# Routed experts of a preLN block: token rows kept as fp16 halves, results scattered by choice, down products in fp16

## What is computed

```python
x = x + attention(layernorm(x))
flat = layernorm(x)                                    # 2048 x 512
_, topk_idx = top_k(flat @ router_w + router_bias, 4)
comb = the 4 softmax scores of a token, divided by their sum
g = silu(einsum('nd,edf->nef', flat, wg))              # f = 128
u = einsum('nd,edf->nef', flat, wu)
routed = einsum('ne,nef,efd->nd', comb, g * u, wd)
x = x + routed + shared                                # shared: 2 dense experts of width 512
```

## Time and profile before

| | us |
|---|---|
| median of 3 runs (lowest, highest) | 1158.7 (1157.71, 1162.43) |
| the profiled execution | 1163.25 |
| its span, first to last instruction | 1161.4 |
| PE busy | 1090.9 (94%) |
| DVE busy | 818.3 (70%) |
| ACT busy | 571.3 (49%) |
| POOL busy | 458.5 (39%) |

### The profile page before, as it was taken

The page is one execution under the profiler, slowest core; times in us unless marked ns, Lnnn a source line. Parts: engine busy times, 40 slices in busy tenths (PEclk is TensorE's granted clock), DMA queues, the critical chain, the costliest instruction groups (busy, mean ns, idle before and its releaser), DMA issues.

```text
span 1161.4 us, 29336 instructions
## 1 busy us (share of the span) xinstructions
PE 1090.9 (94%) x9641; PEld 493.2 (42%) x9641; DVE 818.3 (70%) x1324; ACT 571.3 (49%) x1123; POOL 458.5 (39%) x591
## 2 busy tenths in 40 slices
PE   5995899999999998899999999999999999998998
PEld 3533233333333332455444544544454444543443
DVE  6674899999999994697889345555555554537474
ACT  3311689889889889335303244444444433411010
POOL 5741233344344334205819533333333322227570
PEclk9997899999999999999999999999999999999999
DMA  8176032242232130342000488879887788647561
GB/s 244 40 184 150 19 68 43 49 75 41 44 79 41 42 62 3 135 156 74 1 1 1 162 262 285 240 228 319 246 270 212 217 313 283 192 121 237 177 189 65
DMA packets 76313, 161.67 MB, mean 139 GB/s; under 512 B 18644, under 2 KB 20052, under 8 KB 76260
## 3 DMA queue, kind: packets, MB, share of 16 engines
q1 hardware_dynamic: 42036, 92.72, 27.5%
q0 software_dynamic: 17216, 41.47, 12.4%
q10 hardware_dynamic: 17008, 26.76, 7.8%
HBM read 223.90 MB, written 41.42 MB: 228 GB/s over the span
## 4 chain that ended last, share of the span: by engine, by line
PE 54%; DVE 17%; issue 10%; DMA 7%; ACT 4%; POOL 3%; ACTq 2%; SPq 1%; DVEq 0%; POOLq 0%
PE PS L1423 10%; PE PS L1300 9%; PE PS L1405 7%; DVE maxes L1495 6%; DMA slot_y<-w_att 6%; PE PS L1214 5%; PE PS L1440 5%; PE PS L1095 4%; DVE max_low L1495 4%; PE PS L1163 3%; PE PS L1192 3%; ACTq L1052 2%; ACT att L956 2%; PE PS L1267 2%; PE PS L1383 2%
## 5 line engine op out<-in xcount | busy, mean ns | idle before, releaser
L956 ACT ACTIVATE att<-PS 128x512 f32<-128x512 f32 x576 | 312.5, 595 | 42.7 <-PE PS L1192 35.9
L1214 PE MATMUL PS<-att,v_head 128*32 128x256 f32 (+1 forms) x2560 | 178.7, 370 | 0.9 <-POOL att L761 0.9
L1495 DVE TENSOR_REDUCE maxes<-PS 128x2 f32<-128x1024 f32 (+2 forms) x192 | 172.8, 940 | 3.2 <-PE PS L1100 3.1
L1300 PE MATMUL PS<-XN,att 128*128 128x512 f16 x768 | 167.7, 379 | 4.9 <-DVE w_att L1744 3.7
L1495 DVE TENSOR_REDUCE max_low<-PS 128x2 f32<-128x1024 f32 x128 | 153.3, 1209 | 13.0 <-PE PS L1095 11.1
L875 POOL DMA_INDIRECT w_att<-xn_rows,idx x96 | 98.7, 1028 | 83.0 <-POOL idx L873 78.3
L1095 PE MATMUL PS<-att 48*128 48x512 f16 (+7 forms) x768 | 116.8, 328 | 15.5 <-DMA att<-ring 7.8
L1771 DVE SCALAR_TENSOR_TENSOR XT<-w_att,XT 128x512 f16<-128x512 f32 x96 | 66.4, 692 | 89.9 <-ACT XT L1030 89.9
L761 POOL TENSOR_SCALAR_AFFINE_SELECT att<-att 128x512 f32<-128x512 f32 (+1 forms) x96 | 74.9, 787 | 136.1 <-ACT att L956 135.3
L1192 PE MATMUL PS<-att 50*128 50x512 f16 (+1 forms) x640 | 112.3, 364 | 15.4 <-ACT att L956 13.1
L1036 ACT ACTIVATE w_att<-PS 128x512 f32<-128x512 f32 x96 | 57.3, 597 | 123.2 <-PE PS L1384 49.1
(11 more groups left out here) (188 smaller groups left out, 1625.1 us busy)
## 6 DMA issues: line engine op xcount, KB each, us to landing
ring<-in_L_ffn_wg_dram SPq DMA_DIRECT2D x96, 512.0 KB
XT<-in_L_ffn_wg_dram SPq DMA_DIRECT2D x96, 512.0 KB
ring<-in_L_ffn_wd_dram SPq DMA_DIRECT2D x96, 256.0 KB
XT<-in_L_ffn_wd_dram SPq DMA_DIRECT2D x96, 256.0 KB
slot_y<-w_att ACTq DMA_DIRECT2D x192, 128.0 KB
att<-q_stacks SPq DMA_DIRECT2D x60, 192.0 KB, 3.9
att<-k_stacks SPq DMA_DIRECT2D x60, 96.0 KB, 4.2
xn_rows<-w_att SPq DMA_DIRECT2D x16, 256.0 KB, 2.3
```

The costliest lines, as they stand in the source:

```text
L956: act.activation(probs[:, n0 % RING, u * BANK:(u + 1) * BANK], bank((2 * n0 + u) % EXP_BANKS), ACT.Exp, scale=HD ** -0.5 / QK_SCALE ** 2). ...
L1214: mm = pe.matmul(PS[32 * r:32 * r + 32, at:at + qn], v_head[b][:, kt, :], probs[:, (NS * b + s) % RING, a:a + qn], start=s in (0, NS0), st ...
L1300: mm = pe.matmul(bank(2 * (n % 2) + k), shared_w[:, 2 * k + w, C * s + c, at:at + P], v[:, c, tokens], start=(c == 0 and w == 0 and v is x ...
L1495: last = dve.reduce_max(out, src, AXX)
```

## The change

Four things change; the stages and PE's order stay.

1. **Token rows as halves.** The second layer norm gives rows scaled by 16 (`eps_scaled`, no scale at `x_hi`). ACT writes the high half of each of the 16 row tiles, POOL the low half (`row_low`), and SP stores both side by side in `xn2_rows` (2048 x 1024 fp16, as many bytes as before). A gathered row then holds both halves; `tokens_high` and `tokens_low` are gone, PE turns `xg` as it lands.
2. **Results by choice and token.** POOL scatters the rows of `yb` by an indirect DMA (`scatter_y`) into `choice_y` (8192 x 512, by choice and token); empty slots are skipped. `store_y` on ACT's queue is gone. After the loop SP reads four rows per token by plain DMAs of 1 MB. The table has to tell choice and token: the one-hot products carry a signed code, which DVE takes apart with 8 small operations.
3. **Down products in fp16.** ACT (`down_high`) and DVE (`down_low`) split both experts' down weights (128x1024) in every pair-step; `expert_down` becomes three products of 2 instructions. `turn_hidden` keeps the halves of the hidden values apart (128x256).
4. **Order.** The copy of row numbers moves from POOL to ACT (`next_tokens`), `hidden_turned` from DVE to ACT, and POOL issues gather m+8, then scatter m.

The diff, cut to the loop, the token rows and the results:

```diff
             for t in range(NT):
-                sp.wait_ge(xn2_ready, t + 1)
-                sp.dma_start(xn2_rows[t * P:(t + 1) * P, :], xn2[:, t % 4, :]).then_inc(xn2_stored, 16)
-                if t % 4 == 3:
+                if t % 4 == 1:
                     load_stage(2 + t // 4)
+                sp.wait_ge(row_lo_done, t + 1)
+                sp.dma_start(xn2_rows[t * P:(t + 1) * P, :], row_parts[:, t % 4, :]).then_inc(xn2_stored, 16)
...
-                    wait(sp, e_down, JP * (i - 1) + j + 1)
-                    sp.dma_start(lane_w[n][:, 2, :], wd[bass.ds(code, 1), :, :].rearrange("o f d -> f (o d)"),
-                                 bounds_check="skip_entire_dma").then_inc(lane_down_in[n], 16)
+                    wait(sp, down_lo_done, JP * (i - 1) + j + 1)
+                    sp.dma_start(pair_down[j][:, n % 2, :], wd[bass.ds(code, 1), :, :].rearrange("o f d -> f (o d)"),
+                                 bounds_check="skip_entire_dma").then_inc(pair_down_in[j], 16)
...
+            choices = choice_y.rearrange("(s k m p) d -> s m p k d", s=2, k=TOPK, p=P)
+            def load_choices(t):
+                sp.dma_start(yk[:, t % YK, :, :], choices[t // (NT // 2), t % (NT // 2)]).then_inc(yk_in[t % YK], 16)
+            for done in yb_stored:
+                sp.wait_ge(done, 16 * PAIRS // 2)
+            for t in range(YK):
+                load_choices(t)
             for t in range(NT):
                 sp.wait_ge(mixed, TOPK * (t + 1))
+                if t + YK < NT:
+                    load_choices(t + YK)
...
+            def row_low(t):
+                pool.wait_ge(row_hi_done, t + 1)
+                pool.tensor_tensor(row_parts[:, t % 4, D:2 * D], xn2[:, t % 4, :], row_parts[:, t % 4, 0:D], ALU.subtract)\
+                    .then_inc(row_lo_done, 1)
...
             def gather_tokens(i, j):
                 n = JP * i + j
-                wait(pool, xg_lo_done, n - 3)
-                pool.tensor_copy(idx[:, j:j + 1], tab_t[:, bass.ds(j * LANE_TILES + i, 1)]).then_inc(idx_set, 1)
                 wait_alone(pool, idx_set, n + 1, pool_passed)
                 pool.indirect_dma_start(out=xg[:, j, :], out_offset=None, in_=xn2_rows[:, :],
                                         in_offset=bass.IndirectOffsetOnAxis(ap=idx[:, j:j + 1], axis=0),
                                         bounds_check=NTOK - 1, oob_is_err=False)\
                     .then_inc(xg_in[j], 16)
+            def scatter_y(i, j):
+                n = JP * i + j
+                pool.wait_ge(idx_y_set, n + 1)
+                wait_alone(pool, yb_ready, n + 1, pool_passed)
+                pool.indirect_dma_start(out=choice_y[:, :],
+                                        out_offset=bass.IndirectOffsetOnAxis(ap=idx_y[:, j % 2:j % 2 + 1], axis=0),
+                                        in_=yb[:, j % 2, :], in_offset=None, bounds_check=TOPK * NTOK - 1,
+                                        oob_is_err=False).then_inc(yb_stored[j % 2], 16)
             pool.wait_ge(table_ready, 1)
             pool.wait_ge(xn2_stored, 16 * NT)
             pool.memset(xg[:, :, :].rearrange("p n d -> p (n d)"), 0.0).then_inc(xg_zero, 1)
             pool.wait_ge(xg_zero, 1)
-            for j in range(JP):
-                gather_tokens(0, j)
-            with pool.Fori(1, LANE_TILES) as i:
+            for i in range(2):
                 for j in range(JP):
                     gather_tokens(i, j)
-            for s in yb_stored:
-                pool.wait_ge(s, 16 * PAIRS)
-            for t in range(NT):
-                if t >= YK:
-                    pool.wait_ge(mixed, TOPK * (t - YK + 1))
-                for k in range(TOPK):
-                    pool.indirect_dma_start(out=yk[:, t % YK, k, :], out_offset=None, in_=slot_y[:, :],
-                                            in_offset=bass.IndirectOffsetOnAxis(ap=slot_u[:, k, t:t + 1], axis=0))\
-                        .then_inc(yk_in[t % YK], 16)
+            with pool.Fori(2, LANE_TILES) as i:
+                for j in range(JP):
+                    gather_tokens(i, j)
+                    scatter_y(i - 2, j)
+            for i in range(LANE_TILES - 2, LANE_TILES):
+                for j in range(JP):
+                    scatter_y(i, j)
         @block.scalar
         def _(act):
...
+            def next_tokens(i, j):
+                act.activation(idx[:, j:j + 1], tab_t[:, bass.ds(j * LANE_TILES + i, 1)], ACT.Copy).then_inc(idx_set, 1)
+            def hidden_turned(n, j):
+                act.wait_ge(e_turn, n + 1)
+                wait(act, e_down, n - 1)
+                act.activation(hg[:, j % 2, :], bank(6 + j % 2, 2 * P), ACT.Copy).then_inc(e_turned, 1)
+            def down_high(n, j, i):
+                act.wait_ge(pair_down_in[j], 32 * (i + 1))
+                wait(act, e_down, n - 1)
+                act.activation(down_hi[:, j % 2, :], pair_down[j][:, :, :].rearrange("p l d -> p (l d)"), ACT.Copy,
+                               scale=W_SCALE).then_inc(down_hi_done, 1)
...
+                            next_tokens(i + 1 + (j + 1) // JP, (j + 1) % JP)
                     silu(n, j)
                     e_high(n, j)
-                    if not (first and j < 3):
-                        store_y(i if j == 3 else i - 1, (j + 1) % JP if j < 3 else 0)
-            for k in range(2):
-                tokens_high(k, k, 0)
+                    if not (first and j < 1):
+                        hidden_turned(n - 1, (j - 1) % JP)
+                    down_high(n, j, i)
...
-            def turn_slots(n, k):
-                pe.wait_ge(xg_lo_done, n + 1)
+            def turn_slots(n, k, i):
+                pe.wait_ge(xg_in[k % JP], 16 * (i + k // JP + 1))
                 wait(pe, xgt_ready, n - 1)
                 for c in range(C):
                     at = slice((k % 2) * BANK + c * P, (k % 2) * BANK + (c + 1) * P)
-                    pe.matmul(PS[:, at], xg_hi[:, k % 2, c:D:C], ident_h[:, :], start=True, stop=False)
-                    mm = pe.matmul(PS[:, at], xg_lo[:, k % 2, c:D:C], ident_h[:, :], start=False, stop=True)
+                    pe.matmul(PS[:, at], xg[:, k % JP, c:D:C], ident_h[:, :], start=True, stop=False)
+                    mm = pe.matmul(PS[:, at], xg[:, k % JP, D + c:2 * D:C], ident_h[:, :], start=False, stop=True)
...
+            def expert_down(n, j):
+                pe.wait_ge(down_lo_done, n + 1)
                 pe.wait_ge(e_turned, n + 1)
                 wait(pe, yb_ready, n - 1)
-                for l in range(2):
-                    mm = pe.matmul(PS[l * SUB:(l + 1) * SUB, (4 + j % 2) * BANK:(5 + j % 2) * BANK],
-                                   hg[:, j % 2, l * SUB:(l + 1) * SUB], lane_w[2 * j + l][:, 2, :],
-                                   start=True, stop=True)
+                for v, w in ((0, down_hi), (0, down_lo), (1, down_hi)):
+                    for l in range(2):
+                        mm = pe.matmul(PS[l * SUB:(l + 1) * SUB, (4 + j % 2) * BANK:(5 + j % 2) * BANK],
+                                       hg[:, j % 2, v * P + l * SUB:v * P + (l + 1) * SUB],
+                                       w[:, j % 2, l * D:(l + 1) * D], start=(v == 0 and w is down_hi), stop=v == 1)
                 mm.then_inc(e_down, 1)
             def expert_pairs(i, first, last):
                 for j in range(JP):
                     n = JP * i + j
...
+            def down_low(n, j):
+                dve.wait_ge(down_hi_done, n + 1)
                 wait(dve, e_down, n - 1)
-                dve.tensor_scalar(hg[:, j % 2, :], bank(6 + j % 2, P), 1 / H_SCALE, None, ALU.mult).then_inc(e_turned, 1)
-            def expert_y(n, j, count):
+                dve.scalar_tensor_tensor(out=down_lo[:, j % 2, :], in0=pair_down[j][:, :, :].rearrange("p l d -> p (l d)"),
+                                         scalar=W_SCALE, in1=down_hi[:, j % 2, :], op0=ALU.mult, op1=ALU.subtract)\
+                   .then_inc(down_lo_done, 1)
+            def expert_y(n, j, i, count):
+                wait(dve, yb_stored[j % 2], 16 * count)
+                dve.tensor_copy(idx_y[:, j % 2:j % 2 + 1], tab_y[:, bass.ds(j * LANE_TILES + i, 1)]).then_inc(idx_y_set, 1)
                 dve.wait_ge(e_down, n + 1)
-                wait(dve, yb_stored[j % 2], 32 * count)
-                dve.tensor_copy(yb[:, j % 2, :], bank(4 + j % 2)).then_inc(yb_ready, 1)
...
                     n = JP * i + j
-                    if not (last and j >= JP - 2):
-                        tokens_low(n + 2, j + 2)
                     expert_hidden(n, j)
-                    if not (first and j < 1):
-                        hidden_turned(n - 1, (j - 1) % JP)
                     e_low(n, j)
                     if not (first and j < 2):
-                        expert_y(n - 2, (j - 2) % JP, 2 * i + (j - 2) // 2)
+                        expert_y(n - 2, (j - 2) % JP, i if j >= 2 else i - 1, 2 * i + (j - 2) // 2)
+                    if not (first and j < 1):
```

(2 more changed lines are left out.)

151 lines of the change are left out of this document (88 added, 63 removed).

## The result

The changed kernel took 1182.28 us (median of 4, 1173.36 to 1186.47), the kernel before beside it 1158.2 us (1156.35 to 1162.43). The ratio is 1.0188, 95% interval 1.0155 to 1.0220: slower by 1.9%, 24 us. Forecast were 1144 us, a gain, and a range up to 1176; the time lies above both. The profiled execution took 1181.72 us, and its span is 1180.0 us against 1161.4.

What follows compares the result with a forecast made beforehand. PE's work was taken to bound the loop, with the result buffer's round trip close behind. Loop -12.6, behind it -3, ahead +1 make -14.6 us: 1158.7 becomes 1144 us; own range 1128 to 1160, wider range 1118 to 1176.

Steps and rivals of the forecast that it cites:

- PE's part: Expert loop: down products fall from 1.01 to 0.71 us, PE's floor from 3.68 to 3.38 us a pair-step.
- The added work: Busy time added on ACT and DVE in the loop; all fits under 3.38 us a pair-step, ACT barely.
- The round trip: Loop: from one scatter's landing to a dependent scatter's start through DVE, ACT and POOL, 6.65 us, spanning three pair-steps.
- so a pair-step takes at least (6.6 + L) / 3: Loop: the buffer's trip sets the pair-step when over 3.38 us; forecast 3.67 us, 352.3 us for the loop.
- L: A scatter's time from its start to landing, taken as 4.4 us, between 3.3 and 5.5.
- first rival: PE keeps the lead in the loop: scatters land in under 3.9 us, total 1116 to 1128 us; chance 0.25.
- The scatter behind the gather: POOL's queue in the loop: the scatter DVE waits for is held behind a gather waiting for ACT's row numbers.
- the scatter's round trip eats it all: POOL in the loop: slower from L = 4.8 or 4.9; at 5.5 loop 387 us, total 1179; chance 0.2.
- Around the loop: Behind the loop, first `mix` comes earlier, -3 us; ahead of it, added work costs +1 us.
- Ahead of it: Before the loop: table operations, clearing `xg` and earlier down weights cost +1 us (0 to 2).
- The lower end of the range, 1118: Whole kernel: the range leaving out 2 in 10 starts at PE's floor, 1118 us.
- The landing: Scatter in the loop: skill's rule gave 2.6 us, a hidden trip; the trace's lowest, 3.3, was held to decide.

Runs made afterwards that it cites:

- e9: Changed kernel with four result buffers, scatter issued before gather, and POOL waiting for the up products' end before both: 1128.7 us, ratio 0.9737.
- e11: Changed kernel with fp32 down products, four result buffers, and POOL waiting for the up products' end: 1149.2 us, ratio 0.9905.
- e10: Changed kernel, two result buffers, with `down_low` ahead of the result copy in DVE's order: 1152.6 us, ratio 0.9930.
- e13: Changed kernel, two result buffers, scatter before gather, POOL waiting for the up products' end before both: 1170.5 us, ratio 0.9963.
- e15: e13 with `down_low` ahead of the result copy in DVE's order: 1154.6 us, ratio 0.9834.
- e14: Changed kernel, two result buffers, gather first, with only POOL's wait for the up products' end added: 1211.9 us, ratio 1.0313.
- e6: Changed kernel with results stored by ACT in slot order and POOL's gathers back behind the loop: 1199.5 us, ratio 1.0225.
- e2: Changed kernel with four result buffers instead of two, gather first: 1137.1 us, ratio 0.9694.
- e3: Changed kernel with down products back in fp32, no splits, two result buffers: 1187.6 us, ratio 1.0105.
- e7: Changed kernel with fp32 down products, no splits, and four result buffers: 1182.4 us, ratio 1.0075.
- e4: Changed kernel with scatter before gather and four result buffers: 1166.2 us, ratio 0.9945.
- e8: Changed kernel with four result buffers, gather first, and POOL waiting for the up products' end before both: 1132.2 us, ratio 0.9651.
- e5: Kernel before the change, with four result buffers instead of two: 1165.1 us, ratio 0.9931.
- e1: Changed kernel, two result buffers, with POOL issuing the scatter before the gather: 1168.7 us, ratio 0.9951.

## Why the prediction was wrong, point by point

**PE's part was right.** The down products were forecast at 0.71 us and took 0.77 (822.52 to 823.29), PE's floor at 3.38 and is 3.43. e9 reaches it. Against e11 the part is worth 1.7%, so the first limit was lowered as said.

**The added work was right in size**, from the groups by line, 700 to 950 us (busy us, mean ns):
```profile
L1859 DVE SCALAR_TENSOR_TENSOR XT<-XT 128x1024 f16<-128x1024 f32 x32 | 38.9, 1215 | 0.0
...
L1099 ACT ACTIVATE XT<-ring 128x1024 f16<-128x1024 f32 x32 | 33.7, 1052 | 3.6 <-PE PS L1489 3.5
...
L1093 ACT ACTIVATE w_att<-PS 128x256 f16<-128x256 f32 x62 | 22.6, 365 | 0.0
...
L1087 ACT ACTIVATE idx<-small 128x1 uint32 x62 | 12.3, 198 | 0.0
```
`down_low` 1.22 against 1.22 forecast, `down_high` 1.05 against 1.04, `hidden_turned` 0.37 against 0.38, `next_tokens` 0.20 against 0.2.

**The round trip was right as a path.** The scatter starts 0.31 behind a gather that waits for ACT, and from the landing at 774.65 to the start of the scatter that depends on it 6.69 us pass, where 6.65 were summed:
```profile
780.01 1.02 POOL L911 DMA_INDIRECT w_att<-xn_rows,idx  x1 [2.58 <-ACT idx L1087]
781.34 1.01 POOL L920 DMA_INDIRECT choice_y<-w_att,idx_y  x1 [0.31 <-issue]
```

**The step that failed is "so a pair-step takes at least (6.6 + L) / 3", with one L of 4.4 put in for all.** It has two faults. First, it is a rule of means, and the loop has a floor: a scatter that lands early gives nothing below 3.43, and one that lands late is paid in full. The median pair-step is 3.44, not 3.67; DVE waited for a scatter in 24 of 62 pair-steps, where the forecast had said in most; and of the loss of 388.2 - 96 x 3.43 = 59 us, 48 lie in the 23 steps of over 4.4 us, such as the one behind the landing of 6.70 at 767.82. The prediction said itself, against its first rival, that "every longer landing is felt", and then used the typical one. Over the whole loop DVE stood on 37 scatters, and went on 2.9 to 7.0 us after their start, 5.1 at the median; of the other 57 it is known only that they had landed when DVE came, 4.5 us after their start at the median. So 4.4 may have been near the middle, and what the sum lacked was the spread, with the 6.23 us of the earlier trace rows as a case to be expected. How much of the 36 us between 352.3 and 388.2 each fault made was not separated. Second, `down_low` went into the sum as 1.22 us of length. Its weight is another: it stands behind the wait in DVE's queue, and PE's next products wait for it, so that a wait on DVE becomes a wait of PE. Before, what stood behind `expert_y` had time to spare, and 38.6 us of DVE's waits cost PE next to nothing (4.4 us idle in 250). After, 37.8 us of them cost 28.8. e10 changed this place alone and got 25.5 us of the loop back, more than the change had lost in it, though DVE waited longer; the same exchange won 17 us from e13 to e15.

**The scatter behind the gather was rightly blamed, but not alone.** Turned round it is worth 45 us of loop and half of DVE's waits in the kernels where POOL waits for the products (e14 to e13). But in e6 there is no such scatter, and its loop is as long as that of after: ACT's stores come late as well, and the fp16 part alone makes that dear. So the slower loop has one cause, a trip too long for two buffers under a floor lowered to 3.43, with `down_low` behind the wait, and several edits that each take some of it away.

**The rival "the scatter's round trip eats it all" had the right sign and, at L = 5.5, the right number**, 387 us for 388.2. Its mechanism was right too, in that four buffers win all back (e2) and the order of POOL matters (e13, e14). It had a chance of 0.2, and was priced by the same rule of means, with an L above the middle even of the scatters that DVE stood on, and without the lower clock. That the number agrees is luck, and no support for the rule.

**The fall of the clock was not in the sum.** After 3.38 us of idle PE the up products took 3.16 us, and the granted clock of 775 to 785 us is 0.83 as a mean and 0.50 from 778 to 780, its lower level of 1.2 GHz. PE was busy 221.21 us for 62 pair-steps of 3.43 us, 212.7: 8.5 us in 250 are longer products. The longer stalls here cost more than their length.

**Around the loop.** Behind it the forecast was -3 us, and 132.1 became 129.4, with the first `mix` 10.5 us behind the loop (forecast 10.8):
```profile
1050.55 13.68 PE L1347 MATMUL PS<-XN,att 128*128 128x512 f16 x55
...
1061.01 3.11 DVE L1896 SCALAR_TENSOR_TENSOR X<-ring,small,X 128x512 f32<-128x512 f32 x4 [1.92 <-DMA ring<-choice_y]
```
Ahead of it +1 was forecast and -2.0 measured (662.41 against 664.39). The other kernels started their loops between 660.2 and 665.0, so this is no more than executions differ. (The lower end of the range, 1118, leaves out the 2 us around the loop that the first rival counts, 1116; nothing hangs on it.)

**The landing.** The Trainium skill ("DMA: Bandwidth & Descriptors", section "Anatomy of one DMA — SWDGE (gpsimd) path") would give 2.6 us for a scatter, by an estimate from its figures. The trace does not agree: the six scatters in the chain between 760 and 860 us took 4.81 to 6.70 us to their release, and the shortest of the 37 that DVE stood on took 2.9. The chain picks out late ones, but none of it speaks for a trip that hides.

## What to carry to other kernels

Before a step is put behind a wait in an in-order queue, ask who waits for that step: a wait that cost nothing becomes a stall at full price without getting longer. Where a ring of buffers has little slack, price the late landings one by one against the floor, not the mean one. Buffers come first: with two more, this change is 2.6 to 3.5% faster than the kernel before, where each reordering won less. And compare a kernel with one of another chip only after looking at whether the reference itself changed: here it did, by 13 to 17 us, in a part that the changed kernel no longer has.

## What the runs showed of the hardware

The late signals were not expected. In e3 and e7 ACT's silu started mostly 0.5 to 3.5 us behind the end of PE's up products by the record, and 4.9 us behind it at most in e4. POOL's DMAs stood close to the ends of those products in e3. Three pairs of runs seem to show that POOL's wait for the products removes it: remote waits fell from 14.0 us to none (e2 to e8), from 58.3 to none (e4 to e9) and from 151.2 to none (e7 to e11). They do not show it. The last two pairs set e9 and e11 against another chip, and on theirs no kernel has a remote wait; neither have before and after. All remote waits, the 30.9 us behind e5's loop included, lie in the three batches in which the kernel before took 1174 us. In e8 and e9 the wait hardly acted and POOL was in issue across nearly every end.

Among those three batches two pairs speak for POOL's part: e2 to e8, and e1 to e13, which differ in the wait alone (71.3 to 2.0 us). Against it stands e15, with the wait and 50.2 us. And in after a scatter issued at 852.33 stood across the end of the products, and silu began at 852.51 without delay.
```profile
852.33 1.02 POOL L920 DMA_INDIRECT choice_y<-w_att,idx_y  x1 [0.31 <-issue]
852.51 0.28 ACT L1079 ACTIVATE w_att<-PS 128x128 f32<-128x128 f32 x1 [2.37 <-PE PS L1470]
```
So an issue across the end of the products is not enough. Whether it is the chip, POOL's timing or both together was not separated; e4 and e9, or e7 and e11, on one chip would do it. PE's ends are modelled, and whether the products or only their signals were late can't be told from these records.
